# Strassen's seven block products in a feed-forward layer, in two passes over half of F, on one TensorE

## The chip, the cores and the metric

The kernel runs on one core of one Trainium2 chip. The metric is the device time of one execution in microseconds (us); lower is better. A change of 0.2% or less can't be told from no change for this kernel.

## The reference, cut to what matters

One transformer block with cross-attention: B = 16 batches, S = 512 rows, D = 512 features, F = 2048 hidden features, all float32.

```
x   = query + attention(layer_norm(query), context) @ wo + bo
h   = layer_norm(x) * ln2_g + ln2_b
out = x + gelu(h @ w1 + b1) @ w2 + b2        # w1: 512 x 2048, w2: 2048 x 512
```

The change touches only the last two lines, the feed-forward layer.

## The kernel before

The program has two stages, one after the other. Stage A computes the attention for all batches and writes `x` to the DRAM scratch `x1`. Stage B (`stage_b`, lines 840 to 1194) reads it back and computes the feed-forward layer. TensorE (PE) multiplies in the format fp32r, and every product is made of three: each operand is split into a high part (rounded to that format) and a low part (the rest), and `split_product` (lines 952 to 956) adds high x high, high x low and low x high into one PSUM bank. A "high" is a rounding copy, a "low" is one subtraction of two SBUF tiles. The columns streamed by one matmul are 512 in stage B.

Stage B keeps both parts of `w1` and `w2` in SBUF and goes once over the 16 batches. Per batch:

- **Load.** SP loads the batch twice, as `xn` (for the norm) and as `xr` (for the residual) (lines 939 to 942).
- **Norm and transpose.** DVE computes statistics and normalises `xn` (lines 1032 to 1047), PE transposes it in 16 transposes of 128 columns (`x_transpose`, line 958), ACT writes the high part and DVE the low part of `hT` (lines 1121 and 1049). The scale `ln2_g` is folded into `w1` and the shift into `b1` once, at the start (`scale_w1`, line 1069; `bias_product`, line 988).
- **Hidden tiles.** For each of 16 tiles of 128 hidden features (`hidden`, line 966): 12 matmuls into `bank_f`; ACT applies gelu (line 1146); DVE writes the high part (line 1058) and the low part (line 1060) of the result.
- **Output.** Two tiles later (`output`, line 977): 12 matmuls that add this tile's share to the four banks `bank_o`. After the last tile DVE adds `bank_o` to `xr` (line 1113) and SP stores it (line 945). POOL has added `b2` to `xr` before (line 1190).

So a batch is 16 x 12 + 16 x 12 = 384 matmuls of 512 columns and 16 transposes. Each engine has its own program, in which the first batch, a loop over the middle 14 and the last batch are written out; engines meet only at semaphores, and the instructions of one engine start in the order written. During the first batch the weights are split as they come in: `w1` by ACT and DVE (lines 1126 and 1078), `w2` by ACT and POOL (lines 1130 and 1177).

Lines of stage A that the prediction uses only for their durations: line 410 is its dense products (those of V stream 256 columns), 460 and 425 the attention's, 710 the exponential on ACT.

## Time and profile before

| | us |
|---|---|
| median of 3 runs | 3095.35 (3094.23 to 3096.35) |
| the profiled execution: its own time | 3096.19 |
| its span, first to last instruction | 3094.5 |
| stage A | 0 to 1587 |
| stage B | 1587 to 3094.5 |

Busy over the span: PE 96%, weight load (PEld) 78%, DVE 49%, ACT 37%, POOL 15%; mean granted TensorE clock 0.982. The profiled execution is 0.8 us above the median. Its own time is 1.7 us more than its span.

How to read it: "busy" is the time in which at least one instruction of the engine is under way. Matmuls overlap, so the time of one (398 ns for 512 columns) is longer than the distance from its start to the next one's. The views used below are: the table of stretches (busy time of each engine, granted clock, DMA), the chain of work that ended last, the groups of instructions by line, the order in time of one engine, one line's durations, and the page's list of DMA issues.

### The profile page before, as it was taken

Reading aid. Unit: us, or ns where it says so; the run is one execution under the profiler, and the core shown is the slowest. Engines: PE = TensorE matmul, PEld = TensorE weight load, DVE = VectorE, ACT = ScalarE, POOL = GpSimd, SP = SyncE. Lnnn points to the kernel's source line nnn. Section 1 sums busy time; section 2 is a strip of 40 time slices with the busy share of each in tenths; the row PEclk is TensorE's granted clock in tenths of the full one; section 3 lists DMA queues with packets and bytes.
Section 4 is the critical chain, followed back from the end, with each engine's and each line's share of the span. In section 5 each row is a group of like instructions: output and inputs, shape, how many; then the busy total and the mean of one; then the engine's idle time right before and its main releaser. Section 6 shows DMA issues by size and latency. Waiting matters only on the chain. (4 is left out here: it accounts for less than half of the span.)

```text
span 3094.5 us, 52560 instructions
## 1 busy us (share of the span) xinstructions
PE 2965.2 (96%) x17576; PEld 2408.6 (78%) x17576; DVE 1520.4 (49%) x4100; ACT 1153.1 (37%) x2958; POOL 459.1 (15%) x432
## 2 busy tenths in 40 slices
PE   6999999999999999999979999999999999999999
PEld 5777877778777777777758888888888888888887
DVE  4766666666676666766634333322333322333322
ACT  3655566555666565655622111111111111111111
POOL 1222122211222112222112000000000000000000
PEclk9999999999999999999979999999999999999999
DMA  5766676666666666666522111100111100111100
GB/s 133 122 113 102 111 107 111 115 110 108 107 108 119 112 102 115 103 119 110 89 85 82 41 41 41 41 9 32 41 41 41 41 31 10 41 41 41 41 27 14
DMA packets 123695, 231.89 MB, mean 75 GB/s; under 512 B 10752, under 2 KB 10752, under 8 KB 123648
## 3 DMA queue, kind: packets, MB, share of 16 engines
q1 hardware_dynamic: 123648, 231.28, 37.5%
q8 instruction: 28, 0.46, 0.1%
q14 instruction: 19, 0.16, 0.0%
HBM read 97.02 MB, written 33.55 MB: 42 GB/s over the span
## 5 line engine op out<-in xcount | busy, mean ns | idle before, releaser
L710 ACT ACTIVATE sm<-sm,mins 128x128 f32<-128x128 f32 (+3 forms) x1024 | 571.7, 559 | 606.4 <-DVE mins L574 603.6
L574 DVE CUSTOM_DVE_ANT_0 sm<-bank_s,mask 128x128 f32<-128x128 f32 (+3 forms) x1024 | 480.7, 488 | 451.2 <-PE bank_s L425 440.5
L1146 ACT ACTIVATE g_sb<-bank_f,b1s 128x512 f32<-128x512 f32 x256 | 176.2, 688 | 1173.1 <-PE bank_f L956 1173.1
L1058 DVE CAST g_hi<-g_sb 128x512 fp32r<-128x512 f32 x256 | 113.0, 441 | 866.9 <-ACT g_sb L1146 866.9
L437 PE MATMUL bank_t<-ident,sm 128*128 128x128 f32 x2560 | 424.1, 281 | 53.5 <-ACT pT L520 34.1
L437 PEld LDWEIGHTS bank_t<-ident,sm 128*128 128x128 f32 x2560 | 305.8, 143 | 156.9 <-issue 76.6
L954 PE MATMUL bank_f<-hT_hi,w_hi 128*128 128x512 f32 x1024 | 407.6, 398 | 1.6 <-DVE hT_lo L1052 1.6
L954 PE MATMUL bank_o<-w_hi,g_hi 128*128 128x512 f32 x1024 | 408.0, 398 | 0.0
L956 PE MATMUL bank_f<-hT_hi,w_lo 128*128 128x512 f32 x1024 | 406.7, 397 | 0.0
L955 PE MATMUL bank_f<-hT_lo,w_hi 128*128 128x512 f32 x1024 | 406.4, 397 | 0.0
L956 PE MATMUL bank_o<-w_hi,g_lo 128*128 128x512 f32 x1024 | 406.3, 397 | 0.0
L955 PE MATMUL bank_o<-w_lo,g_hi 128*128 128x512 f32 x1024 | 405.6, 396 | 0.0
L425 PE MATMUL bank_s<-stack 96*128 96x128 f32 (+3 forms) x1024 | 357.3, 390 | 6.5 <-DMA stack<-st_lo 5.8
L520 DVE COPY pT<-bank_t 128x384 f32<-128x384 f32 (+1 forms) x576 | 326.9, 568 | 0.5 <-PE bank_t L437 0.5
L1190 POOL TENSOR_TENSOR xr<-xr,b_row 128x512 f32<-128x512 f32 x64 | 81.3, 1301 | 1213.2 <-DMA xr<-x_scratch 1213.2
L954 PEld LDWEIGHTS bank_f<-hT_hi,w_hi 128*128 128x128 f32 x1024 | 193.4, 189 | 48.3 <-issue 2.0
L956 PEld LDWEIGHTS bank_f<-hT_hi,w_lo 128*128 128x128 f32 x1024 | 193.7, 189 | 47.4
L955 PEld LDWEIGHTS bank_f<-hT_lo,w_hi 128*128 128x128 f32 x1024 | 193.9, 189 | 46.8
L956 PEld LDWEIGHTS bank_o<-w_hi,g_lo 128*128 128x128 f32 x1024 | 193.1, 189 | 46.6
L955 PEld LDWEIGHTS bank_o<-w_lo,g_hi 128*128 128x128 f32 x1024 | 193.0, 188 | 46.2
L954 PEld LDWEIGHTS bank_o<-w_hi,g_hi 128*128 128x128 f32 x1024 | 192.8, 188 | 45.5
L792 POOL TENSOR_TENSOR oT_lo<-rT,oT_hi 128x512 fp32r<-128x512 f32 x64 | 82.3, 1286 | 814.6 <-ACT oT_hi L724 814.6
(108 smaller groups left out, 4486.5 us busy)
## 6 DMA issues: line engine op xcount, KB each, us to landing
stack<-st_hi SPq DMA_DIRECT2D x256, 256.0 KB, 5.6
xt<-in_x SPq DMA_DIRECT2D x32, 1024.0 KB, 5.3
stack<-st_lo SPq DMA_DIRECT2D x128, 256.0 KB, 7.2
c_raw<-in_ctxT SPq DMA_DIRECT2D x64, 256.0 KB, 6.0
x_scratch<-xt SPq DMA_DIRECT2D x64, 256.0 KB, 2.0
xn<-x_scratch SPq DMA_DIRECT2D x16, 1024.0 KB, 7.7
xr<-x_scratch SPq DMA_DIRECT2D x16, 1024.0 KB, 5.6
out<-xr SPq DMA_DIRECT2D x64, 256.0 KB, 2.1
```

The source lines that it names most:

```text
L425: mm = pe.matmul(bank_s[n % BANKS_S][:, off:off + w], stack[0:96, g % 2, 0, r, P * qt:P * qt + P], stack[0:96, g % 2, 1, r, 0:w], start=Tr ...
L437: mm = pe.transpose(bank_t[n % 2][:, P * c:P * c + P], sm[:, n % SLOTS_S, P * c:P * c + P], ident[:])
L520: copy(out, src).then_inc(moved[n % 2], 1)
L574: op = V.tensor_tensor_reduce(sm[:, n % SLOTS_S, off:off + w], bank_s[n % BANKS_S][:, off:off + w], mask[:, 512 - w:512], 1.0, 0.0, ALU.ad ...
L710: op = A.activation(row, row, ACT.Exp, bias=mins[:, g % 2, c:c + 1], scale=-1.0, accum_out=sums[:, g % 2, c:c + 1])
L792: G_.tensor_tensor(out=oT_lo[:, g % NG, :], in0=rT[:], in1=oT_hi[:, g % NG, :].bitcast(F32), op=ALU.subtract).then_inc(oT_done, 1)
L954: pe.matmul(o, lh, rh, start=first, stop=False)
L955: pe.matmul(o, lh, rl, start=False, stop=False)
L956: return pe.matmul(o, ll, rh, start=False, stop=last)
L1058: V.tensor_copy(g_hi[:, f % RING_H, :], g_sb[:, f % 2, :]).then_inc(g_hi_ok, 1)
L1146: A.activation(g_sb[:, f % 2, :], bank_f[f % 2][:], ACT.Gelu, bias=b1s[:, f:f + 1], scale=1.0).then_inc(gelu, 1)
L1190: G_.tensor_tensor(out=xr[:, t, :], in0=xr[:, t, :], in1=b2_row[:], op=ALU.add).then_inc(xr_ok, 1)
```

## The change

Matrices are cut into 2 x 2 blocks, and each block product of the feed-forward layer is done by the Strassen-Winograd scheme: seven products of blocks in place of eight, with sums of blocks before and after. Both layers are done so. To make room in SBUF for the seven block operands of `w1` and `w2`, the work is done in two passes over all batches, each with one half of F: pass 0 adds the first half's share of the output and `b2` to `x` and stores it back into the DRAM scratch; pass 1 loads that, adds the second half's share and stores the result. The normalised and transposed `hT` is computed in pass 0, stored to a new DRAM scratch (`h_scratch`) and loaded again in pass 1. One batch in one pass is called a unit here; there are 32.

What a unit does:

- PE, first layer (`layer1`): 14 steps in the order of `STEPS`, as (d, place): d is the half of the unit's hidden features, place one of the seven products. A step is 2 x 2 x 3 = 12 matmuls of 256 columns. In pass 0 four groups of four transposes for the next batch follow steps number 9 to 12; all four use one bank, `bank_t`.
- PE, second layer (`layer2`): k = 0 to 6, the seven products, each in two halves h = 0, 1 of 12 matmuls of 256 columns. `layer2(0)` stands before the last step of the first layer. k = 0, 2, 4 and 6 share `bank_x2`, so k = 4 waits until the output of k = 2 was added to `xr` (`sum_out(2)`).
- ACT: 6 copies of PSUM blocks to `g`, 16 gelus of 128 x 256, 14 highs of the second layer's left operands (`a_high`), 7 highs of the next unit's `h` (`h_high`), in pass 0 also 4 scaled copies that make `hT`.
- DVE: 6 additions PSUM + SBUF (`add`), 8 sums of SBUF blocks (`a_sum`), 8 lows (`a_low`), 4 sums and 4 lows for the next unit's `h` (`h_parts`, stages 0 to 4), 7 additions PSUM + SBUF to `xr` (`sum_out`); in pass 0 also the norm of the next batch.
- POOL: 6 lows (`a_low` of k = 3, 4, 6) and 3 lows of `h` (B22, B21, T3); in pass 0 the four additions of `b2` and the inverse root.
- The weights' block operands are made on the way, in the first unit of pass 0, the last unit of pass 0 and the first unit of pass 1 (`w1_parts`, `w2_parts`: each 7 highs on ACT, 4 sums and 4 lows on DVE, 3 lows on POOL). Their raw blocks are loaded into `xr`, `g` or `xn`, one after the other, as `raw_used` allows.

All blocks are 128 x 512 elements. The core of the diff:

```diff
-def stage_b(nc, x1, w1, w2, vecs, b2, out):
...
+def stage_b(nc, x1, h_scratch, w1, w2, vecs, b2, out):
...
+    STEPS = [(0, 0), (0, 1), (0, 2), (0, 3), (0, 4), (0, 5), (1, 0), (0, 6),
+             (1, 1), (1, 2), (1, 3), (1, 4), (1, 5), (1, 6)]
+    X_AFTER = {9: 0, 10: 1, 11: 2, 12: 3}
...
+    A_LOW_V = [(0, 0), (1, 0), (0, 1), (1, 1), (2, 0), (2, 1), (5, 0), (5, 1)]
+    A_LOW_P = [(3, 0), (3, 1), (4, 0), (4, 1), (6, 0), (6, 1)]
...
+    T_HIGH = ["B11", "B22", "T1", "T3", "B21", "T2", "T4"]
+    T_LOW_V, T_LOW_P = ["B11", "T1", "T2", "T4"], ["B22", "B21", "T3"]
...
+    PLACE1_B = ["B11", "T1", "B21", "T2", "B22", "T3", "T4"]
...
+        b_hi = sb("b_hi", [P, 7, 2, C], F32R)
+        b_lo = sb("b_lo", [P, 7, 2, C], F32R)
...
+        raw = [xr, g[:, 4:8, :], xr, xr, xn, xn, xn, xn]
...
+        def over_batches(eng, body):
...
+            body(0, 0, True, False)
             with eng.Fori(1, B - 1) as c:
+                body(c, 0, False, False)
+            body(B - 1, 0, False, True)
+            body(B, 1, True, False)
+            with eng.Fori(B + 1, 2 * B - 1) as c:
+                body(c, 1, False, False)
...
+            def raw_used(u):
+                sp.wait_ge(w_lo_v, 4 * (u + 1))
+                sp.wait_ge(w_lo_p, 3 * (u + 1))
...
+            def store_h(m):
+                sp.wait_ge(hT_ok, m * KT + KT)
+                sp.dma_start(one(h_v, m), hT[:]).then_inc(h_stored, 16)
...
+            def body(c, ph, first, last):
+                b = c - ph * B
+                if ph == 0 and not last:
+                    sp.wait_ge(x_t, c * KT + KT)
+                    sp.dma_start(xn[:], one(x_v, b + 1)).then_inc(xn_in, 16)
...
+                    sp.wait_ge(stored, c * 32 + 32)
...
+            def x_transpose(m, f, bank):
+                if f == 0:
+                    pe.wait_ge(xn_ok, m * QT + QT)
+                if f > 0 and bank is bank_t:
+                    pe.wait_ge(hT_ok, m * KT + f)
+                for t in range(QT):
+                    mm = pe.transpose(bank[:, P * t:P * t + P], xn[:, t, P * f:P * f + P], ident[:])
...
+            def block_product(o, lh, ll, rh, rl, opens):
+                pe.matmul(o, lh, rh, start=opens, stop=False, skip_group_check=True)
+                pe.matmul(o, lh, rl, start=False, stop=False, skip_group_check=True)
+                return pe.matmul(o, ll, rh, start=False, stop=True, skip_group_check=True)
...
+            def layer1(c, ph, first, d, at_place):
...
+                if at_place == 6:
+                    pe.wait_ge(added, at(c, ADDS, (d, "C22")))
+                for m in range(2):
+                    cols = slice(P * (2 * d + m), P * (2 * d + m) + P)
+                    for kt in range(2):
+                        mm = block_product(bank[:, C * m:C * m + C], w1_hi[:, at_place, kt, cols],
+                                           w1_lo[:, at_place, kt, cols], b_hi[:, at_place, kt, :],
+                                           b_lo[:, at_place, kt, :], at_place < 3 and m == 0 and kt == 0)
+                mm.then_inc(step1, 1)
...
+            def layer2(c, ph, first, k):
...
+                if k == 4:
+                    pe.wait_ge(summed, at(c, OUTPUTS, 2))
...
+                    if (k, h) in A_LOW_V:
+                        pe.wait_ge(a_lo_v, at(c, A_LOW_V, (k, h)))
+                    else:
+                        pe.wait_ge(a_lo_p, at(c, A_LOW_P, (k, h)))
...
+            def body(c, ph, first, last):
+                for n, (d, place) in enumerate(STEPS):
+                    if n == 13:
+                        layer2(c, ph, first, 0)
+                    layer1(c, ph, first, d, place)
+                    if n in X_AFTER and ph == 0 and not last:
+                        x_transpose(c + 1, X_AFTER[n], bank_t)
+                for k in range(1, 7):
+                    layer2(c, ph, first, k)
...
+            def t_parts(n, q, hi, lo, hi_ok, sum_ok, lo_v, lo_p, stage):
+                if stage == 0:
+                    dve.wait_ge(hi_ok, n * 7 + 1)
+                    low(lo("B11"), q["B11"], hi("B11"), lo_v)
+                if stage == 1:
+                    V.tensor_tensor(q["B11"], q["B12"], q["B11"], ALU.subtract).then_inc(sum_ok, 1)
+                    V.tensor_tensor(q["B12"], q["B22"], q["B12"], ALU.subtract).then_inc(sum_ok, 1)
+                if stage == 2:
+                    dve.wait_ge(hi_ok, n * 7 + 3)
+                    low(lo("T1"), q["B11"], hi("T1"), lo_v)
+                    dve.wait_ge(lo_p, n * 3 + 1)
+                    dve.wait_ge(sum_ok, n * 4 + 1)
+                    V.tensor_tensor(q["B22"], q["B22"], q["B11"], ALU.subtract).then_inc(sum_ok, 1)
+                if stage == 3:
+                    dve.wait_ge(lo_p, n * 3 + 2)
+                    dve.wait_ge(sum_ok, n * 4 + 3)
+                    V.tensor_tensor(q["B21"], q["B21"], q["B22"], ALU.subtract).then_inc(sum_ok, 1)
+                    dve.wait_ge(hi_ok, n * 7 + 6)
+                    low(lo("T2"), q["B22"], hi("T2"), lo_v)
+                if stage == 4:
+                    dve.wait_ge(hi_ok, n * 7 + 7)
+                    low(lo("T4"), q["B21"], hi("T4"), lo_v)
...
+            def h_parts(m, ph, stage):
+                if stage == 1 and ph == 0:
+                    dve.wait_ge(h_stored, m * 16 + 16)
...
+            def a_low(c, k, h):
+                dve.wait_ge(a_hi_ok, at(c, A_HIGH, (k, h)))
+                low(a_part(a_lo, k, h), a_source(k, h), a_part(a_hi, k, h), a_lo_v)
...
+                dve.wait_ge(step2, at(c, HALVES, (k, 1)))
+                o = xr[:, 2 * i:2 * i + 2, C * j:C * j + C]
+                V.tensor_tensor(o, bank[:].rearrange("p (t n) -> p t n", t=2), o, ALU.add).then_inc(summed, 1)
...
+            def body(c, ph, first, last):
+                norm = ph == 0 and not last
+                more = ph == 0 or not last
+                if ph == 0 and first:
+                    w2_parts(2, 0, 0)
...
+                add(c, 0, "C11")
+                if norm:
+                    layer_norm_stats(c + 1, 0)
+                    layer_norm_stats(c + 1, 1)
+                add(c, 0, "C12")
+                a_low(c, 0, 0)
+                if norm:
+                    layer_norm_stats(c + 1, 2)
+                add(c, 0, "C22")
+                if norm:
+                    layer_norm_stats(c + 1, 3)
+                a_sum(c, "S1", 0)
+                a_low(c, 1, 0)
+                if norm:
                     for t in range(QT):
+                        normalise(c + 1, t)
+                a_sum(c, "S2", 0)
+                if ph == 0 and first:
+                    w2_parts(3, 0, 1)
+                if ph == 0 and last:
+                    w1_parts(4, 1, 0)
+                if ph == 1 and first:
+                    w2_parts(7, 1, 1)
+                add(c, 1, "C11")
+                add(c, 1, "C12")
+                a_low(c, 0, 1)
+                add(c, 1, "C22")
+                if more:
+                    h_parts(c + 1, ph, 0)
+                a_sum(c, "S1", 1)
+                a_low(c, 1, 1)
+                sum_out(c, ph, 0)
+                a_sum(c, "S2", 1)
+                a_low(c, 2, 0)
+                a_low(c, 2, 1)
+                if more:
+                    if ph == 1 or last:
+                        dve.wait_ge(hT_in, (c - B) * 16 + 32)
+                    h_parts(c + 1, ph if not last else 1, 1)
+                    h_parts(c + 1, ph, 2)
+                a_sum(c, "S3", 0)
+                sum_out(c, ph, 1)
+                a_sum(c, "S3", 1)
+                a_sum(c, "S4", 0)
+                a_sum(c, "S4", 1)
+                if more:
+                    h_parts(c + 1, ph, 3)
+                sum_out(c, ph, 2)
+                a_low(c, 5, 0)
+                sum_out(c, ph, 3)
+                a_low(c, 5, 1)
+                if more:
+                    h_parts(c + 1, ph, 4)
+                for k in (4, 5, 6):
+                    sum_out(c, ph, k)
+                if ph == 0 and last:
+                    w1_parts(5, 1, 1)
...
+            def body(c, ph, first, last):
...
+                    h_high(c + 1, "B11")
+                a_high(c, 1, 1)
+                if more:
+                    h_high(c + 1, "B22")
+                a_high(c, 2, 0)
+                activate(c, ph, 1, "C21")
+                a_high(c, 2, 1)
+                if more:
+                    h_high(c + 1, "T1")
+                    h_high(c + 1, "T3")
+                a_high(c, 3, 0)
+                if more:
+                    h_high(c + 1, "B21")
+                a_high(c, 3, 1)
+                if more:
+                    h_high(c + 1, "T2")
+                a_high(c, 4, 0)
+                a_high(c, 4, 1)
+                if more:
+                    h_high(c + 1, "T4")
...
+            def body(c, ph, first, last):
...
+                if ph == 0 and not last:
                     inverse_root(c + 1)
...
+                    pool.wait_ge(xr_in, c * 16 + 16)
+                    for t in range(QT):
+                        G_.tensor_tensor(out=xr[:, t, :], in0=xr[:, t, :], in1=b2_row[:], op=ALU.add).then_inc(xr_ok, 1)
+                if more:
+                    h_low(c + 1, "B22")
+                a_low(c, 3, 0)
+                a_low(c, 3, 1)
+                if more:
+                    h_low(c + 1, "B21")
+                a_low(c, 4, 0)
+                if more:
+                    h_low(c + 1, "T3")
+                a_low(c, 4, 1)
+                a_low(c, 6, 0)
+                a_low(c, 6, 1)
...
```

## Rows read from the trace of the kernel before

**Rows 1.** Stretches: us, busy by engine (instructions), PEclk, DMA share, GB/s.

```profile
1587.00:3094.50 1507.50, 1490.16 (x6528) 1205.73 (x6528) 467.41 (x872) 226.43 (x329) 119.55 (x87) 0.99 0.11 39
1803.39:1894.84 91.45, 91.45 (x402) 73.84 (x401) 27.87 (x53) 13.16 (x20) 6.28 (x5) 1.00 0.10 35
```

**Rows 2.** Chain that ended last, stage B: start us, us, what.

```profile
1609.95 0.77 PE bank_f L954
...
1711.93 0.87 PE bank_x L963 x8
...
1803.39 0.87 PE bank_x L963 x8
...
1894.84 0.87 PE bank_x L963 x8
```

**Rows 3.** PE in order of time, full clock: start us, us, engine, line, what.

```profile
101.92 0.28 PE L410 MATMUL bank_d<-wv_hi,cT_hi 128*128 128x256 f32 x1
...
103.22 0.28 PE L410 MATMUL bank_d<-wv_hi,cT_lo 128*128 128x256 f32 x1
...
1803.23 1.03 PE L963 MATMUL bank_x<-identb,xn 128*128 128x128 f32 x8
...
1804.34 0.39 PE L955 MATMUL bank_o<-w_lo,g_hi 128*128 128x512 f32 x1
...
1806.67 0.39 PE L956 MATMUL bank_o<-w_hi,g_lo 128*128 128x512 f32 x1
```

**Rows 4.** Groups by line, each shape apart: busy us, mean ns, idle before.

```profile
L1146 ACT ACTIVATE g_sb<-bank_f,b1s 128x512 f32<-128x512 f32 x256 | 176.2, 688 | 1173.1 <-PE bank_f L956 1173.1
L1060 DVE TENSOR_TENSOR g_lo<-g_sb,g_hi 128x512 fp32r<-128x512 f32 x256 | 178.3, 697 | 8.8
L1046 DVE TENSOR_SCALAR xn<-xn,mvb,rstdb 128x512 f32<-128x512 f32 x64 | 35.5, 558 | 2.6 <-POOL rstdb L1167 2.6
L1190 POOL TENSOR_TENSOR xr<-xr,b_row 128x512 f32<-128x512 f32 x64 | 81.3, 1301 | 1213.2 <-DMA xr<-x_scratch 1213.2
...
L710 ACT ACTIVATE sm<-sm,mins 128x512 f32<-128x512 f32 x256 | 185.2, 723 | 215.1 <-DVE mins L574 213.1
L710 ACT ACTIVATE sm<-sm,mins 128x256 f32<-128x256 f32 x256 | 126.4, 494 | 0.0
L724 ACT CAST oT_hi<-rT 128x512 fp32r<-128x512 f32 x64 | 38.7, 604 | 2.2 <-DVE rT L584 2.2
```

**Rows 5.** In order of time, three queues: several in one row start one behind another.

```profile
1810.88 2.48 DVE L1113 TENSOR_TENSOR xr<-bank_o,xr 128x512 f32<-128x512 f32 x4 [1.44 <-PE bank_o L956]
1803.86 1.07 ACT L1123 CAST hT_hi<-bank_x 128x512 fp32r<-128x512 f32 x2 [2.55 <-PE bank_x L963]
1822.29 5.05 POOL L1190 TENSOR_TENSOR xr<-xr,b_row 128x512 f32<-128x512 f32 x4 [85.24 <-DMA xr<-x_scratch]
```

**Rows 6.** DVE and POOL in order of time, where they meet in the first batch.

```profile
1693.51 1.79 DVE L1060 TENSOR_TENSOR g_lo<-g_sb,g_hi 128x512 fp32r<-128x512 f32 x1
1695.23 1.51 DVE L1046 TENSOR_SCALAR xn<-xn,mvb,rstdb 128x512 f32<-128x512 f32 x1
...
1693.47 5.66 POOL L1190 TENSOR_TENSOR xr<-xr,b_row 128x512 f32<-128x512 f32 x4
```

**Rows 7.** The page's DMA issues: KB each, us to landing.

```profile
xn<-x_scratch SPq DMA_DIRECT2D x16, 1024.0 KB, 7.7
xr<-x_scratch SPq DMA_DIRECT2D x16, 1024.0 KB, 5.6
```

**Rows 8.** PE in order of time behind two idle times, stage A.

```profile
37.40 0.39 PE L410 MATMUL bank_d<-wv_hi,cT_hi 128*128 128x256 f32 x1 [2.16 <-DVE wv_lo L606]
...
38.16 0.41 PE L410 MATMUL bank_d<-wv_hi,cT_lo 128*128 128x256 f32 x1
...
41.15 0.41 PE L410 MATMUL bank_d<-wv_lo,cT_hi 128*128 128x256 f32 x1
...
116.94 0.76 PE L410 MATMUL bank_d<-xnT_hi,wq_hi 128*128 128x512 f32 x1 [1.70 <-DVE xnT_lo L552]
```

More of the change, by code:

```diff
@@ L950, in _ @@
+            over_batches(sp, body)
+            sp.wait_ge(stored, 64 * B + 32)
         @block.tensor
         def _(pe):
[L952 to L964 removed]
@@ new lines, in _ @@
+            pe.sem_inc(step1, len(STEPS))
+            pe.sem_inc(step2, len(HALVES))
+            pe.wait_ge(consts, 1)
+            for f, bank in enumerate((bank_x2, bank_y2, bank_z2, bank_t)):
+                x_transpose(0, f, bank)
+            def body(c, ph, first, last):
[7 more added lines that the diff above has]
+                    layer2(c, ph, first, k)
@@ new lines, in h_high, with copy @@
+            def h_high(m, name):
+                act.wait_ge(step1, before(m, STEPS, (1, PLACE1_B.index(name))))
+                t_high(m + 1, quarters(hT), lambda name: b_hi[:, PLACE1_B.index(name), :, :], b_hi_ok, b_sum_ok, name)
+            def copy(c, d, name):
+                place, bank, to = {"P1": (0, bank_x[d], "C11"), "P5": (1, bank_y, "C22"), "U2": (3, bank_x[d], "C12")}[name]
+                act.wait_ge(step1, at(c, STEPS, (d, place)))
+                A.copy(g_block(d, to), bank[:].rearrange("p (m s) -> p m s", m=2)).then_inc(copied, 1)
@@ new lines, in activate @@
+            def activate(c, ph, d, name):
+                rows = "C1 C2".split().index(name[:2])
+                if name == "C21":
+                    act.wait_ge(step1, at(c, STEPS, (d, 6)))
+                else:
+                    act.wait_ge(added, at(c, ADDS, (d, name)))
+                for m in range(2):
+                    to = g_block(d, name)[:, m, :]
+                    f = 2 * KT + 8 * ph + 4 * rows + 2 * d + m
+                    op = A.activation(to, bank_x[d][:, C * m:C * m + C] if name == "C21" else to, ACT.Gelu,
+                                      bias=vec[:, f:f + 1], scale=1.0)
+                op.then_inc(gelu, 1)
@@ L1183, in body @@
-            def body(c, first, last):
-                if first:
-                    for wc in range(WC):
-                        w2_low(wc)
-                    inverse_root(1)
-                pool.wait_ge(xr_in, c * 16 + 16)
-                for t in range(QT):
-                    G_.tensor_tensor(out=xr[:, t, :], in0=xr[:, t, :], in1=b2_row[:], op=ALU.add).then_inc(xr_ok, 1)
-                if not last and not first:
-                    inverse_root(c + 1)
-            over_chunks(pool, body)
+            w1_parts(0, 0, 0)
```

609 lines of the change are left out of this document (395 added, 214 removed).

## The prediction

> **What bounds it now.** The table of stretches says that stage B takes 1507.5 of 3094.5 us, and that in a middle batch PE is busy for all of its 91.45 us at full clock, DVE for 27.9, ACT for 13.2, POOL for 6.3 [rows 1]. The chain of waits shows the same from the other side: its pieces in stage B are matmuls one behind another, and the transposes come back every 91.45 us [rows 2]. So only fewer or shorter matmuls help, and PE has no idle time to lose: what the other engines add is free only while it stays under PE. The first batch is dearer: 102.0 us from its first matmul to its transposes [rows 2], where a middle batch needs 84.1 (a period less the 24 matmuls and 16 transposes that close it, 7.4); so the weights and the start cost 17.9 us.
>
> **PE's work.** The distance between matmuls is read at full clock: ten distances of 512 columns take 2.33 us; eleven of 256 columns 1.30 us, so 118.2 ns each [rows 3]. Eight transposes take 0.88 us with the step back to matmuls (1803.23 to 1804.34, less one matmul), so 16 cost 1.8 [rows 3]. That leaves (91.45 - 1.8) / 384 = 233.5 ns per 512 columns over a whole batch. After: 672 x 0.1182 = 79.4 us, plus 2.0 for the transposes in four groups. PE's work falls from 91.45 to 81.4, by 10.1 us a batch, 161 us in all. Splitting 512 columns into 256 costs nearly nothing: the weights' load keeps up in the V products, which load as often. A pass-1 unit is 336 x 0.1182 = 39.7 us of PE, a pass-0 unit 41.6.
>
> **The other engines.** DVE: 0.69 us for 128 x 512, and one behind another every 0.60 (four in 2.48). ACT: 0.60 for a high, 0.58 for a copy, every 0.49 (two in 1.07); a gelu of 256 columns 0.49, as the exponential of that shape from SBUF (of 512 columns it takes 0.72 and the gelu 0.69). POOL: 1.29, every 1.25 (four in 5.05) [rows 4, 5]. Per unit: DVE 37 x 0.60 = 22 (pass 0: 27), ACT 20 (22), POOL 9 x 1.25 = 11 (17). All are under 39.7: no engine is full, and if throughput were all, the change would give its 161 us. What decides is the order, because PE now meets the others many times a unit, and they meet one another.
>
> **DVE against POOL.** In the first batch, a DVE low (both inputs in SBUF), 0.69 elsewhere, started 0.04 behind the first of POOL's four additions and took 1.79: it ended 0.54 after POOL's first one did (1693.47 + 1.29 = 1694.76; 1695.30). DVE's next, a normalise (0.56 elsewhere), took 1.51 and ended about 0.27 after POOL's second. The four additions took 5.66 in place of 5.05: the 0.6 are DVE's turn [rows 5, 6]. So in this trace they take turns by whole instructions. The Trainium skill (SBUF — State Buffer, section Who interferes with whom) says of which this holds: a VectorE instruction with two SBUF inputs and a GpSimd instruction that reads SBUF block each other for the whole instruction, one with a single SBUF input isn't touched; the trace agrees for the one low it can show. The page speaks against this change, which puts 24 two-input DVE instructions beside 9 POOL lows in a unit; by it the sum is 3425, without it 3127 (below). I take turns for all of them, as the row shows for the same kind of instruction: a pair costs 1.25 + 0.54 = 1.79, less 0.04 of overlap. DVE's additions with an input in PSUM I leave free; if they took turns too, the two in the stretch below would cost 1 to 2 us a unit.
>
> **The walk of a unit.** I went through the five queues in the order of the diff, starting each instruction when its queue is free and its last wait over, with the durations above and as allowances, which no row fixes closely, 0.04 to 0.15 us from one engine to the next and 0.11 more when PE starts again (0.05 more each way is worth 20 us in all). It repeats after one unit. The long stretch is the end of the second layer. Call T the end of DVE's low of (k 2, h 1). DVE then has, before it may add the output of k = 2 (for which k = 4 waits, bank_x2): sums T1 and T3, low T1, sum T2 (to T + 2.6), sums S3(0), S3(1), S4(0), S4(1), sum T4, low T2, and two additions to xr. POOL is released at T + 2.4 by the high of (3, 0), and from there has six lows in a row: (3, 0), (3, 1), B21, (4, 0), T3, (4, 1). Each of DVE's six meets one of them: 6 x 1.75 = 10.5. Sum T4 also has to wait for B21. The addition of k = 2 ends at T + 13.55, PE starts k = 4 at T + 13.7. In that time PE has only the halves (2, 1), (3, 0), (3, 1): 4.3 us. Idle: 0.4 at k = 2, 1.6 and 0.2 at k = 3 (POOL's lows), 6.5 at k = 4, and 0.45 for four starts: 9.2. **A pass-1 unit takes 48.9.**
>
> **Pass 0** has in addition: the load of xn is issued only behind the last store of the unit before (1.6 us after PE began the unit), lands 5.6 later [rows 7], and DVE wanted it at 5.1; the addition C22 comes late and step (0, 6) waits 1.2. The normalise starts behind it, together with POOL's four additions of b2, and three of its four take turns with them: PE waits 4.6 for the first transposes. The four groups share one bank: 0.7 and 0.65 for ACT's copies. With the 8.3 of the second layer and 0.8 for seven starts: 16.3. **A pass-0 unit takes 57.9.** A batch is then 57.9 + 48.9 = 106.8 where it was 91.45. DVE's wait for the store of hT costs nothing: it lands 4 to 5.6 us after its issue and DVE comes 6.3 after it (at 7.7, PE would lose 1.4 a unit).
>
> **The ends.** To the first matmul 27 (now 23). First unit 84, 26 more than a middle one: two blocks of w2 come one after the other (5.6 load, then some 10 of sums and lows) and stand in DVE's queue before the additions that PE waits for. The boundary unit 58.7 (two blocks of w1 in place of the norm). First unit of pass 1 74.1, 25 more, again two blocks of w2. Sum of stage B: 27 + 84 + 14 x 57.9 + 58.7 + 74.1 + 14 x 48.9 + 43.8 (the last, nothing to prepare) + 1 = 1784; with 1587 before it 3371.
>
> **The clock.** Behind an idle time of 2.16 us the matmuls of 256 columns stand 0.214 us apart from 38.16 to 41.15 (14 distances in 2.99), where 0.107 would be full speed by their columns: the granted clock is at 1.2 in place of 2.4 GHz, for some 3.4 us. Behind 1.70 us the first matmul takes 0.76 in place of 0.39, the same fall [rows 8]. A unit's 6.5 us are longer than either, and PE is then the bound until the next unit's middle. I take 1.7 us for each of 32 units: 54. Bounds: none (0), or twice in a pass-0 unit (+27). Sum: 3371 + 54 = 3425 span, 3427 with the 1.7 around it; the profiled execution is 0.8 above the median: 3426.
>
> **Rivals.**
> 1. *Turns and half clock*, as above: 3426. Own range 3290 (DVE at 0.60 and 0.51, which the walk prices at -78, and little half clock) to 3485 (xn landing in 7.7, +30, and two falls a unit). For it: [rows 6, 8]. Chance 0.65; with full clock all through, 3371: 0.12.
> 2. *No turns*: the low of row 6 was an accident. The same walk without them gives 49.1 and 43.3 a unit (idle 1.5 at k = 4, 1.35 at the transposes) and 3127 in all; up to 3180 with half clocks. Slower still, since the queues' order alone eats the gain. Against: three instructions in [rows 6] agree to 0.1 us. Chance 0.10.
> 3. *Faster*: the queue behind T drains in time. The place is `sum_out(2)` against k = 4: if it ends within PE's 4.3 us, and the norm likewise, PE never waits: 1587 + 23 + 16 x 81.4 + 18 + 25 + 5 = 2960. The other ends cost some 37 us more than now, 2.3 a batch, so it decides at an idle time of 10.1 - 2.3 = 7.8 us a batch; the walk has 25. For it: no engine is over 70% full by throughput. Against: six POOL lows at 1.25 alone are 7.5 us, longer than 4.3. Chance 0.11.
> 4. *Seven blocks are no cheaper than eight*: in long runs 256 columns are held up by the weights' load. At the 184 ns a load that PEld's busy time gives (73.84 / 401, [rows 1]), PE's work alone would be 125.6 a batch: about 3680. Against: the 12 in a row at 118 [rows 3]. Chance 0.02.
>
> **The numbers.** 3426 is the likeliest. The range 3150 to 3480 leaves out the faster case, the lower half of rival 2, and rival 4. Faster by over 0.2% (what can be told from no change) 0.11, slower 0.86, between 0.03.
>
> **What would show it.** Right: PE busy some 80% in stage B and waiting longest for DVE's addition to xr; DVE's two-input instructions at 1.2 to 1.8 us in the mean of their groups, POOL's lows at 1.6 to 1.8; 256-column matmuls 118 ns apart; granted clock near 0.96 in stage B. Wrong: POOL's lows at 1.29 (no turns), PE's idle under 8 us a batch, a clock of 1.00 behind the long waits, or matmuls over 125 ns apart.

## The result, and the profile after

The changed kernel takes 3465.7 us (median of 4 runs, 3464.2 to 3466.9) where the kernel before took 3095.7 in the same session: a ratio of 1.119 (95% interval 1.118 to 1.121). It is slower by 370 us; 3426 was forecast, with a range of 3150 to 3480. The profiled execution has a span of 3464.9.

The stretches of [rows 1] in the profile after, first all of stage A and all of stage B, then one unit of pass 0 and one of pass 1 (columns as there: PE, weight load, DVE, ACT, POOL, granted clock, DMA share, GB/s):

```profile
0.00:1587.00 1587.00, 1475.47 (x11048) 1202.22 (x11048) 1052.76 (x3228) 927.11 (x2629) 339.86 (x345) 0.98 0.63 109
1587.00:3464.90 1877.90, 1463.55 (x11008) 1431.55 (x11008) 1140.68 (x1456) 784.34 (x1497) 582.06 (x395) 0.90 0.19 67
2193.47:2254.87 61.40, 47.21 (x355) 45.70 (x354) 37.85 (x50) 24.89 (x47) 20.76 (x14) 0.92 0.20 68
2702.06:2753.04 50.98, 43.28 (x339) 42.55 (x338) 30.02 (x37) 21.99 (x43) 13.56 (x9) 0.93 0.18 63
```

Stage A is what it was. Stage B takes 1877.9 in place of 1507.5. PE works 1463.6 us there: less than the 1490.2 of before even with the stretches at half clock counted in, and it now waits for the other 414. DVE has gone from 467 to 1141 us of busy time, POOL from 120 to 582.

What PE waited for in stage B (engine, line, tile <- releaser: us in total, times, longest us). Before, the middle batches had no such waits: PE was busy for all of their 91.45 us [rows 1]:

```profile
PE bank_x L1080 <- DVE xr L1304: 191.3, 31, 6.2
...
PE bank_t L1069 <- DVE xn L1192: 65.0, 15, 4.5
...
PE bank_z L1080 <- POOL a_lo L1560: 44.5, 31, 1.5
```

The first row is the wait of k = 4 for DVE's addition of k = 2, 31 times 6.2 us; the second is the transposes' wait for the normalise, 4.3 us each; the third k = 3 behind POOL's lows. These are the three places that the walk named, at nearly the lengths it gave (6.5, 4.6, 1.6). Left out above are the waits of the first units (47.4 us in 6 waits for ACT's copies, L1439) and one more that the walk named, step (0, 6) behind DVE's addition of C22 (L1267): 21.1 us in 14 waits, 1.5 each, where it had 1.2.

The groups that answer to [rows 4] (busy us, mean ns), POOL's lows, DVE's sums and its normalise, and one of its additions with an input in PSUM:

```profile
L1560 POOL TENSOR_TENSOR a_lo<-g,a_hi 128x512 fp32r<-128x512 f32 x192 | 287.6, 1505 | 352.2 <-ACT a_hi L1464 352.0
...
L1560 POOL TENSOR_TENSOR b_lo<-hT,b_hi 128x512 fp32r<-128x512 f32 x96 | 151.0, 1573 | 603.5 <-ACT b_hi L1421 603.5
...
L1284 DVE TENSOR_TENSOR s_sums<-g,s_sums 128x512 f32<-128x512 f32 x64 | 110.3, 1762 | 0.0
...
L1279 DVE TENSOR_TENSOR g<-g 128x512 f32<-128x512 f32 x64 | 93.2, 1456 | 0.0
...
L1304 DVE TENSOR_TENSOR xr<-bank_x,xr 128x512 f32<-128x512 f32 x128 | 87.8, 686 | 164.1 <-PE bank_x L1082 164.1
...
L1192 DVE TENSOR_SCALAR xn<-xn,mvb,rstdb 128x512 f32<-128x512 f32 x64 | 71.2, 1171 | 1.1 <-POOL rstdb L1557 1.1
...
L1243 DVE TENSOR_TENSOR hT<-hT 128x512 f32<-128x512 f32 x32 | 55.8, 1744 | 1.2 <-POOL b_lo L1560 1.2
```

The same kind of instruction costs 0.69 us where nothing meets it [rows 4], and 1.74 to 1.76 in the mean of the two groups whose every member meets POOL (s_sums, L1284, and hT, L1243). Additions with one input in PSUM (L1304) stay at 0.69 in the midst of the same stretch. One such stretch in a pass-0 unit, in order of time:

```profile
2169.99 1.46 DVE L1196 TENSOR_TENSOR a_lo<-s_sums,a_hi 128x512 fp32r<-128x512 f32 x2
...
2173.94 1.78 DVE L1279 TENSOR_TENSOR g<-g 128x512 f32<-128x512 f32 x1
2175.64 0.68 DVE L1304 TENSOR_TENSOR xr<-bank_y,xr 128x512 f32<-128x512 f32 x1
2176.24 1.18 DVE L1279 TENSOR_TENSOR g<-g 128x512 f32<-128x512 f32 x1
2177.35 3.45 DVE L1284 TENSOR_TENSOR s_sums<-g,s_sums 128x512 f32<-128x512 f32 x2
2180.72 1.74 DVE L1243 TENSOR_TENSOR hT<-hT 128x512 f32<-128x512 f32 x1
2182.39 1.75 DVE L1196 TENSOR_TENSOR b_lo<-hT,b_hi 128x512 fp32r<-128x512 f32 x1
2184.07 0.68 DVE L1304 TENSOR_TENSOR xr<-bank_x,xr 128x512 f32<-128x512 f32 x1
```

```profile
2173.90 2.98 POOL L1560 TENSOR_TENSOR a_lo<-g,a_hi 128x512 fp32r<-128x512 f32 x2 [4.38 <-ACT a_hi L1464]
2176.84 1.75 POOL L1560 TENSOR_TENSOR b_lo<-hT,b_hi 128x512 fp32r<-128x512 f32 x1
...
2181.88 1.71 POOL L1560 TENSOR_TENSOR a_lo<-g,a_hi 128x512 fp32r<-128x512 f32 x1
```

```profile
2184.80 0.58 PE L1080 MATMUL bank_x<-w_hi,a_hi 128*128 128x256 f32 x1 [6.17 <-DVE xr L1304]
```

T, the end of DVE's low of (2, 1), is 2169.99 + 1.46 = 2171.45 here. DVE's six meetings with POOL are the rows of 1.78, 1.18, 3.45 (two instructions), 1.74 and 1.75 in the first list, POOL's six lows run from 2173.90 to 2183.59 in the second (two of them left out), and PE's first matmul of k = 4 begins at T + 13.35, where T + 13.7 was forecast.

### The profile page after: what moved, and what is told of

It reads as the page before. It is cut to its first block, busy times and chain, and to the rows that moved or that the text cites. A ratio compares the mean times of both kernels' runs of the same rounds, so it can differ in the third digit from the quotient of the medians.

```text
span 3464.9 us, 66386 instructions
## 1 busy us (share of the span) xinstructions
PE 2939.0 (85%) x22056; PEld 2633.8 (76%) x22056; DVE 2193.4 (63%) x4684; ACT 1711.5 (49%) x4126; POOL 921.9 (27%) x740
## 4 chain that ended last, share of the span: by engine, by line
PE 24%; DVE 18%; issue 5%; ACT 4%; DMA 3%; DVEq 0%; SPq 0%; POOL 0%; ACTq 0%
PE bank_x L1080 5%; PE bank_x L1081 5%; PE bank_x L1082 5%; DVE s_sums L1284 3%; DMA xn<-x_scratch 3%; DVE g L1279 2%; DVE xr L1304 2%; PE bank_y L1080 2%; PE bank_y L1081 2%; PE bank_y L1082 2%; DVE xn L1192 2%; DVE hT L1243 1%; ACT a_hi L1464 1%; DVE b_lo L1196 1%; ACT b_hi L1421 1%
## 5 line engine op out<-in xcount | busy, mean ns | idle before, releaser
L1080 PE MATMUL bank_x<-w_hi,a_hi 128*128 128x256 f32 x1024 | 331.2, 323 | 192.6 <-DVE xr L1304 191.3
L1080 PEld LDWEIGHTS bank_x<-w_hi,a_hi 128*128 128x128 f32 x1024 | 229.3, 224 | 202.8 <-DVE xr L1304 197.5
L1560 POOL TENSOR_TENSOR a_lo<-g,a_hi 128x512 fp32r<-128x512 f32 x192 | 287.6, 1505 | 352.2 <-ACT a_hi L1464 352.0
L1080 PE MATMUL bank_x<-b_hi,w_hi 128*128 128x256 f32 x1024 | 305.7, 299 | 78.9 <-ACT g L1439 47.4
L1081 PE MATMUL bank_x<-w_lo,a_hi 128*128 128x256 f32 x1024 | 321.4, 314 | 0.0
L1082 PE MATMUL bank_x<-w_hi,a_lo 128*128 128x256 f32 x1024 | 319.1, 312 | 0.0
L1081 PE MATMUL bank_x<-b_lo,w_hi 128*128 128x256 f32 x1024 | 300.8, 294 | 0.0
L1082 PE MATMUL bank_x<-b_hi,w_lo 128*128 128x256 f32 x1024 | 300.7, 294 | 0.0
L1081 PEld LDWEIGHTS bank_x<-w_lo,a_hi 128*128 128x128 f32 x1024 | 230.6, 225 | 0.0
L1082 PEld LDWEIGHTS bank_x<-w_hi,a_lo 128*128 128x128 f32 x1024 | 229.2, 224 | 0.0
```

The lines of the kernel that those rows point to most:

```text
L1080: pe.matmul(o, lh, rh, start=opens, stop=False, skip_group_check=True)
L1081: pe.matmul(o, lh, rl, start=False, stop=False, skip_group_check=True)
L1082: return pe.matmul(o, ll, rh, start=False, stop=True, skip_group_check=True)
L1560: G_.tensor_tensor(out=out_, in0=value, in1=high.bitcast(F32), op=ALU.subtract).then_inc(sem_, 1)
```

## The experiments

Each was timed against the kernel before on the same chip. The walk of the prediction, now with 1.9 us of half clock behind each of PE's waits over 1.7 us, gives 3459 for the changed kernel; the forecasts below are differences from that.

**1. The addition of k = 2 put earlier in DVE's queue.**

```diff
                 sum_out(c, ph, 1)
+                sum_out(c, ph, 2)
                 a_sum(c, "S3", 1)
...
-                sum_out(c, ph, 2)
                 a_low(c, 5, 0)
```

> DVE's addition of the output of k = 2 stands right behind that of k = 1, ahead of the sums S3(1), S4(0), S4(1), sum T4 and low T2; nothing else is changed, and the same is computed. Turns with the half clock (my theory; the walk of the record with 1.9 us of half clock behind each idle time over 1.7 us gives 3459 for the changed kernel, 3466 was measured): the wait of k = 4 goes from 6.5 to 2.0 us and is then one for POOL's low of (4, 0), a second of 1.9 us may stand at (4, 1); a pass-1 unit takes 47.3 in place of 51.0, in all 3351, so 108 less than the changed kernel's walk: 3358. Rival A, no turns, POOL is only slow by itself: the wait for this addition would be 1.5 us long, and moving it gives at most 1.5 us a unit: 3415 or more. Rival B, what is lost is lost to the clock alone: a unit's half clock stays as long as any wait is left, and no more than the 4 us of idle time a unit is gained with the clock still at 0.90.

Measured: 3360.1 us, ratio 1.0845 (1.083 to 1.086); 3358 was expected. What PE waited for in stage B:

```profile
PE bank_x L1080 <- POOL a_lo L1560: 102.7, 62, 1.9
...
PE bank_x L1080 <- DVE xr L1304: 16.2, 27, 0.6
```

The 31 waits of 6.2 us are gone, and 62 of at most 1.9 for POOL's low stand in their place, twice a unit. The first pass-1 units take 47.5 (from one store of xr to the next), the later ones 48.7 and 47.0 in turn. Rival A falls, since 105 us were gained where it allowed 50. Rival B falls by the clock: stage B has a granted clock of 0.94 in place of 0.90. The time alone would not have told, for 105 us are 3.3 a unit and B allowed 4. This place in the queue was worth 105 us: PE's waits at k = 4 fell by 72 in all (191.3 to 102.7 + 16.2), and most of the rest is half clock that is gone.

Behind these waits the clock does not always fall. In the unit around 2780 the matmuls behind a wait of 1.87 us are 0.12 us apart; in the unit around 3065 those behind one of 1.86 us fall to 0.21 apart after the second distance.

**2. The additions of b2 moved to pass 1.**

```diff
-                    if ph == 0:
-                        dve.wait_ge(xr_ok, c * QT + QT)
+                    if ph == 1:
+                        dve.wait_ge(xr_ok, (c - B) * QT + QT)
...
-                if ph == 0:
+                if ph == 1:
                     if first:
                         pool.wait_ge(b2_in, 16)
```

> POOL's four additions of b2 to xr are made in pass 1 in place of pass 0, so they no longer stand beside the normalise; the same is computed, and the number of instructions stays. Turns: the wait of the transposes in pass 0 falls from 4.7 to 1.5 us and its half clock goes with it; a pass-0 unit 56.6 in place of 61.1, a pass-1 unit 51.8 in place of 50.8 (its own DVE instructions meet the four additions); in all 3410 by the walk whose value for the changed kernel is 3459, so 49 less: 3417. Rival, no turns: the normalise is late because its data are (the wait is there for the load of xn), and nothing changes: 3466, with DVE's normalise at 1.17 us in the mean as now.

Measured: 3417.2, ratio 1.1035 (1.102 to 1.105); 3417 was expected. DVE's normalise:

```profile
L1192 DVE TENSOR_SCALAR xn<-xn,mvb,rstdb 128x512 f32<-128x512 f32 x64 | 31.5, 555 | 1.1 <-POOL rstdb L1557 1.1
```

0.555 us each, as in [rows 4], where it was 1.17 (above), and PE's wait for it at bank_t falls from 65.0 to 16.5 us in all: the load was not what made it late.

**3. PE kept busy through the wait of k = 4.**

```diff
+                if k == 4:
...
+                    fill(48)
```

(`fill` runs 48 matmuls of 256 columns from w2_hi into bank_t; in pass 0 it waits first until ACT has read that bank)

> Ahead of the wait of k = 4, in every unit, PE runs 48 more matmuls of 256 columns on weights that lie ready, into bank_t, which nobody reads then (48 x 0.118 = 5.7 us, where the wait is 6.2). They compute nothing that is used. The clock: if an idle PE is what takes the clock to one half, the fall at k = 4 goes away in both passes; the matmuls behind it stand 0.12 us apart at once, the granted clock over stage B goes from 0.90 to 0.96 or more, and the time falls by about 1.9 x 30 = 57 us to 3410 (3400 to 3425). Rival: the half clock does not hang on the idle time at k = 4 (it comes with the load on the chip, or costs less than I think): 3466 or more, and a clock of 0.90.

Measured: 3410.9, ratio 1.1015 (1.0996 to 1.103), 55 below the changed kernel; 3410 was expected. Stage B:

```profile
1587.00:3408.10 1821.10, 1586.35 (x12544) 1552.55 (x12544) 1141.37 (x1456) 784.20 (x1497) 584.62 (x395) 0.96 0.20 69
```

The granted clock is 0.96 in place of 0.90, although every engine but PE has the same work as before. So the half clock at k = 4 is the consequence of PE's idle time, and costs 55 / 32 = 1.7 us a unit. In the changed kernel it can be seen in PE's own rows behind the wait:

```profile
2185.61 0.41 PE L1080 MATMUL bank_x<-w_hi,a_hi 128*128 128x256 f32 x1
...
2188.81 0.37 PE L1080 MATMUL bank_x<-w_hi,a_hi 128*128 128x256 f32 x1
```

Between these two there are 15 distances of 0.213 us, which is 1.2 GHz for 256 columns; from 2189.02 on they are 0.12 apart, at 2.4 GHz.

**4. POOL's lows of the second layer in two halves.**

```diff
-                low(a_part(a_lo, k, h), a_source(k, h), a_part(a_hi, k, h), a_lo_p)
+                for m in range(2):
+                    op = G_.tensor_tensor(out=a_part(a_lo, k, h)[:, m, :], in0=a_source(k, h)[:, m, :],
+                                          in1=a_part(a_hi, k, h)[:, m, :].bitcast(F32), op=ALU.subtract)
+                op.then_inc(a_lo_p, 1)
```

> POOL makes each of its six lows of the second layer as two instructions of 128x256 in place of one of 128x512; the same is computed, in the same order. Turns by whole instructions: DVE gets in after each half, so two of its instructions go by in the time of one low; DVE's two-input groups fall from 1.46 to 1.76 us to about 1.1 to 1.3, the wait of k = 4 goes from 6.5 to 2.0, that of k = 3 from 1.6 to 2.1, a pass-1 unit takes 48.4, in all 3384 by the walk whose value for the changed kernel is 3459, so 75 less: 3390. Rival A, no turns (POOL and DVE slow each other down in proportion, by sharing bandwidth): the halves take as much time together as the whole does, DVE's instructions stay at 1.5 to 1.75 us, and the time is 3466 or, with a fixed cost for each of 6 more POOL instructions a unit, up to 3490.

Measured: 3426.0, ratio 1.106 (1.104 to 1.109). 40 us are gained, where turns by whole instructions gave 75 and a sharing of bandwidth none.

```profile
L1284 DVE TENSOR_TENSOR s_sums<-g,s_sums 128x512 f32<-128x512 f32 x64 | 75.4, 1217 | 0.0
...
L1279 DVE TENSOR_TENSOR g<-g 128x512 f32<-128x512 f32 x64 | 60.8, 950 | 0.0
```

```profile
L1586 POOL TENSOR_TENSOR a_lo<-g,a_hi x384: 715/1168/1257, 1682.8 to 3415.5; 128x256 fp32r<-128x256 f32 x192
```

```profile
PE bank_x L1080 <- DVE xr L1304: 75.9, 31, 3.0
...
PE bank_z L1080 <- DVE xr L1304: 62.8, 31, 2.1
```

(The third row gives the least, median and longest duration of POOL's halves in ns, the last two are PE's waits.) DVE's two-input sums fell from 1.76 and 1.46 to 1.22 and 0.95 us: it does get in between the halves. But a half takes 0.72 at the least, more than half of a whole low's 1.29 [rows 4], and 1.17 in the median, so the two take longer than the whole low did here (1.50). The wait of k = 4 stays at up to 3.0 where 2.0 was expected; the one at k = 3 is 2.1 long, as expected, but for DVE's addition and not for POOL's low. The direction is the turns'; the size was missed.

**5. All nine lows on DVE, near their old places.** POOL's body loses its nine calls and DVE's gets them; `t_op` is one instruction of the old `h_parts`, and the counts that PE waits for change over with them.

```diff
+                    t_op(c + 2, H_Q, H_HI, H_LO, b_hi_ok, b_sum_ok, b_lo_v, B_LOW_V, "sT2")
+                a_low(c, 3, 0)
                 a_sum(c, "S3", 0)
                 sum_out(c, ph, 1)
+                a_low(c, 3, 1)
                 a_sum(c, "S3", 1)
                 a_sum(c, "S4", 0)
                 a_sum(c, "S4", 1)
...
-                a_low(c, 3, 0)
-                a_low(c, 3, 1)
```

> All nine of POOL's lows of a unit (six of the second layer, B22, B21, T3 of h) are made by DVE, each put into DVE's queue near where its high is ready; the rest of the order and POOL's four additions of b2 stay. The same is computed. Turns: a low on POOL costs 1.25 us there and holds one of DVE's for as long, on DVE it costs 0.60: so DVE gets nine more instructions and its unit still becomes shorter. By the walk the wait of k = 4 goes from 6.5 to 4.0 us (DVE is now simply full of work there), k = 3 keeps 1.2 to 1.5, a pass-1 unit takes 47.7, a pass-0 unit 58.1, in all 3361. Signs: no DVE two-input group over 0.72 us beside the normalise. Rival, no turns: DVE loses what POOL did for it, 9 x 0.6 = 5.4 us more in front of the additions that PE waits for, and the time rises over 3466.

Measured: 3367.6, ratio 1.088 (1.086 to 1.090); 3361 was expected. DVE's groups:

```profile
L1198 DVE TENSOR_TENSOR a_lo<-g,a_hi 128x512 fp32r<-128x512 f32 x256 | 172.3, 683 | 0.2
...
L1198 DVE TENSOR_TENSOR a_lo<-s_sums,a_hi 128x512 fp32r<-128x512 f32 x192 | 139.3, 726 | 81.3 <-ACT a_hi L1519 78.3
...
L1194 DVE TENSOR_SCALAR xn<-xn,mvb,rstdb 128x512 f32<-128x512 f32 x64 | 71.3, 1173 | 1.1 <-POOL rstdb L1614 1.1
```

The engine that already had the longest queue was given nine more instructions a unit and the kernel became 98 us faster. All of DVE's groups of this shape with two SBUF inputs are at 0.68 to 0.73 in the middle units; the normalise alone, which still meets POOL's additions of b2, is at 1.17.

**6. Everything on DVE and the queues in a new order.** Beyond run 5, b2 is added by DVE in pass 1, the load of xn is issued a unit earlier, and DVE's and ACT's bodies are reordered. DVE's queue from the low of (2, 1) on, as it now stands:

```python
                a_low(c, 2, 1)
                a_low(c, 3, 0)
                a_sum(c, "S4", 1)
                a_low(c, 3, 1)
                sum_out(c, ph, 1)
                a_low(c, 4, 0)
...
                sum_out(c, ph, 2)
...
                a_low(c, 5, 0)
                a_low(c, 4, 1)
                sum_out(c, ph, 3)
...
                a_low(c, 5, 1)
                a_low(c, 6, 0)
...
                sum_out(c, ph, 4)
```

Where lines are left out, a sum or a low of h fills in. S3(0), S3(1) and S4(0) come earlier, ahead of low (2, 1), and the last three lows of h stand around the addition of k = 5. ACT's highs were reordered likewise, those of the second layer ahead of those of h that nobody needs yet.

> A version meant to beat both: all lows on DVE as in the run before, the four additions of b2 on DVE too and in pass 1, DVE's and ACT's queues put into an order found with the walk (each addition to xr right when its product is done, the sums and lows of the first layer's next operand filled in behind), and xn loaded one unit earlier. The same is computed. Turns gone, order mended: by the walk PE has no wait over 0.3 us in a middle unit, a pass-0 unit takes 41.7 and a pass-1 unit 39.7, the first units of the passes 68 and 65, in all 2980: 0.962 of the kernel before. DVE is at 78 to 85% there. Rival A: seven products of 256 columns are dearer on PE than 118.2 us per thousand (the changed kernel shows 0.1195 to 0.12 apart in places), which adds up to 1.5%: 3015. Rival B: a full DVE makes each handover late by a little, with 20 handovers a unit of 0.1 us each: 3045. Slower than 3095 would say that the order's gain is not what the walk holds it for.

Measured: **3011.7 us, ratio 0.973 (0.971 to 0.974)**: faster than the kernel before by 86 us and than the changed one by 454. Stage B and a pass-1 unit:

```profile
1587.00:3010.40 1423.40, 1346.95 (x11008) 1338.22 (x11008) 1086.32 (x1808) 782.56 (x1497) 57.62 (x43) 0.97 0.26 89
2627.22:2667.54 40.32, 40.32 (x338) 40.32 (x337) 30.87 (x52) 22.00 (x44) 0.00 (x0) 1.00 0.22 78
```

PE is busy for all of the 40.32 us of the unit, at full clock, with DVE at 30.9 beside it. 40.32 / 336 = 120.0 ns a matmul, not 118.2: rival A of the expectation, +19 us over the kernel. A pass-0 unit takes 43.0 where 41.7 was expected: the pitch (the distance from one matmul to the next) again, +0.6, and 0.7 for the transposes and small waits. The dear units are the boundary unit (47.4 from one store of xr to the next) and the first of pass 1 (66.7).

**7. The same order with the nine lows back on POOL.**

> The run before with one thing undone: the nine lows are on POOL again, in the same order, all else in the new order. The same is computed. Turns: POOL's lows each hold one of DVE's sums or lows; by the walk a pass-1 unit takes 44.6 and a pass-0 unit 46.6, PE waits 1.9 us for DVE's low of the second layer, with half clock behind it, in all 3133, that is 153 above the run before. Rival, no turns: DVE has nine instructions fewer and PE has no wait: 2958, a little below the run before.

Measured: 3057.7, ratio 0.9875 (0.986 to 0.989): 46 us above run 6, where strict turns gave 153 and none gave -22, and still 40 us faster than the kernel before. PE's waits for POOL's lows are 23.5 us in all, those for DVE's lows 16.3 (7.4 in run 6). The trace shows one place where the walk was too dear. DVE, then POOL, in order of time:

```profile
2659.21 0.68 DVE L1310 TENSOR_TENSOR s_sums<-g,s_sums 128x512 f32<-128x512 f32 x1
2659.81 0.68 DVE L1201 TENSOR_TENSOR a_lo<-s_sums,a_hi 128x512 fp32r<-128x512 f32 x1
2660.41 0.68 DVE L1310 TENSOR_TENSOR s_sums<-g,s_sums 128x512 f32<-128x512 f32 x1
2661.02 0.68 DVE L1330 TENSOR_TENSOR xr<-bank_y,xr 128x512 f32<-128x512 f32 x1
```

```profile
2659.26 6.00 POOL L1623 TENSOR_TENSOR a_lo<-g,a_hi 128x512 fp32r<-128x512 f32 x3 [26.23 <-ACT a_hi L1525]
```

POOL's low came 0.05 us behind DVE's sum at 2659.21, and DVE's next two followed it at their usual 0.60. So it was POOL that waited: its three lows took 6.00 us in place of 3.75. Taken singly they are 3.00, 1.30 and 1.78 us: the first ended at 2662.26, which is its usual 1.25 behind the start of DVE's addition with a PSUM input (2661.02). The walk had DVE wait at each meeting. That the new order also has more slack for the waits that are left is my reading, and no run separates the two.

**8. By hand.** As run 6, but with ACT's queue untouched and DVE's only mended at single places.

> The changed kernel with the single steps put together by hand, and ACT's queue left as it is: all lows on DVE, b2 added by DVE in pass 1, xn loaded a unit earlier, each addition to xr put right behind its product, and the lows T1, T2, T3, T4 of h behind the last lows of the second layer. The same is computed. With nobody on POOL and DVE at 0.60 an instruction, the walk (with 120 ns a matmul, as e6_reordered showed) gives 49.7 for a pass-0 unit and 48.9 for a pass-1 unit, 3256 in all: six waits a unit of 0.6 to 1.7 us, most for DVE's lows, are left because ACT's order still hands DVE its highs late. e6_reordered differs from it only in the order of DVE's and ACT's queues. If taking POOL off and earlier additions were nearly all of it, the time would be close to e6_reordered's 3012, under 3080.

Measured: 3234.7, ratio 1.044 (1.042 to 1.046); 3256 was expected. Run 6 is 223 us faster with the same instructions on the same engines: that much is the order of DVE's and ACT's queues. Reordering the two together doesn't say how much is due to each.

**9. Spare POOL work beside run 6.**

```diff
+                for n, (k, h) in enumerate([(3, 0), (3, 1), (4, 0), (5, 0), (4, 1), (5, 1), (6, 0), (6, 1), (6, 1)]):
+                    pool.wait_ge(a_hi_ok, at(c, A_HIGH, (k, h)))
...
+                    G_.tensor_tensor(out=spare[:], in0=b2_row[:], in1=b2_row[:], op=ALU.subtract)
```

> e6_reordered with nine spare POOL instructions of 128x512 in each unit, where e7_reordered_pool has its lows: they subtract b2 from itself into a tile nobody reads, two SBUF inputs, and no engine waits for them. What is computed stays. So any time above e6_reordered's 3012 is what POOL costs DVE by being in its way, with POOL's own lateness left out. Theory A, strict turns (each DVE two-input instruction that meets POOL waits for it, as the walk has it): 3290. Theory B, who is there first keeps the path: DVE's instructions that follow one another at 0.60 hold POOL off until one with an input in PSUM or a gap comes, and DVE waits only where POOL came first: by the walk with that rule 3052 (3040 to 3070), POOL's instructions at 1.7 us in the mean with some near 3. Theory C, e7_reordered_pool's 46 us were PE waiting for POOL's own lows and DVE loses nothing: 3012.

Measured: 3188.9, ratio 1.0295 (1.028 to 1.031), 177 above run 6. Theory C falls: work that nobody waits for costs 5.5 us a unit, by being in DVE's way. PE's waits for DVE's additions to xr and its lows are 136 us in all (70.9, 47.7, 12.1 and 5.6), where run 6 has 7.4. It costs more than run 7's lows did, although the spare instruction is shorter (1.04 us at the least): DVE now has the nine lows as well. A is 101 too dear and B 137 too cheap, and the rows say what lies between. DVE, then POOL:

```profile
2670.25 0.68 DVE L1311 TENSOR_TENSOR s_sums<-g,s_sums 128x512 f32<-128x512 f32 x1
...
2672.66 0.68 DVE L1202 TENSOR_TENSOR a_lo<-g,a_hi 128x512 fp32r<-128x512 f32 x1
2673.26 0.68 DVE L1331 TENSOR_TENSOR xr<-bank_y,xr 128x512 f32<-128x512 f32 x1
2673.86 0.93 DVE L1202 TENSOR_TENSOR a_lo<-g,a_hi 128x512 fp32r<-128x512 f32 x1
2674.71 1.52 DVE L1202 TENSOR_TENSOR b_lo<-hT,b_hi 128x512 fp32r<-128x512 f32 x1
```

```profile
2670.39 12.54 POOL L1694 TENSOR_TENSOR spare<-b_row 128x512 f32<-128x512 f32 x7 [30.39 <-ACT a_hi L1538]
```

POOL asked at 2670.39, 0.14 behind a DVE sum. Five two-input instructions of DVE, from 2670.25 to 2672.66, then ran at 0.60 us apart; the first with an input in PSUM came at 2673.26. From there on DVE's take 0.93 and 1.52, as these two do. POOL's first took 3.86 us by itself, which is 1.04 from 2673.21 on: it came in with DVE's PSUM addition, as in run 7. In both places DVE kept POOL out as long as it had not been made to wait itself; once POOL had been let in, they took turns. That this is the rule everywhere is not shown.

## Why the prediction was right, and where it was not

**PE's work.** 672 matmuls a batch are cheaper than 384 of 512 columns, as said; run 6, at 3011.7, shows 86 us of it (its first units keep the rest). The price was 118.2 ns, read off eleven distances; over whole units it is 120.0 (run 6): 16 x 672 x 1.8 ns = 19 us too low.

**Turns.** Right, in kind and nearly in size: 1.74 to 1.76 us for DVE's instructions that all meet POOL (1.79 less 0.04), PSUM inputs free. POOL's lows were to be at 1.6 to 1.8 and are at 1.50 and 1.57; the first of a row comes before DVE and takes 1.27 (the one at 2173.90). Rival 2 (no turns) falls with runs 2, 5 and 9. Where DVE is first, the walk was wrong: it had DVE wait at each meeting, and in runs 7 and 9 DVE's instructions kept POOL out while they followed one another.

The Trainium skill (SBUF — State Buffer, section Who interferes with whom) states an exclusive lock of the shared ports for a VectorE instruction with two SBUF inputs and a GpSimd instruction that reads SBUF, and the trace after agrees, down to the exemption of additions with a PSUM input (0.686 us). It exempts an instruction with one SBUF input only outside the two-port modes, and names `tensor_scalar` among the operations that can enter them; the prediction left this condition out. The normalise is such an instruction and does take turns: 1.51 us in [rows 6], 1.17 in the profile after and 0.555 in run 2, where POOL's additions were moved away. Whether it ran in a two-port mode no run shows. The forecast did not suffer, since the walk counted three of its four as meeting POOL.

**The walk.** The three waits stand where it put them. A unit was to take 57.9 and 48.9 without the clock; measured are 61.45 and 51.16 (means of 14 units in each pass), the boundary unit 61.9 for 58.7 and the first unit of pass 1 78.6 for 74.1, from one store of xr to the same of the next unit. The walk took 5.6 us for the load of xn, where [rows 7] has 7.7 for it, without saying why; the profile after has 5.7, so this held by a choice that was not argued. What a unit takes over the walk is the clock's, less 0.6 for the pitch:

**The clock** is the term that was furthest off. I took 54 us, one fall a unit at k = 4, and run 3 confirms it: 55. But pass 0 has a second one behind the transposes' wait, which I had as a bound and not in the sum. PE in the profile after:

```profile
2155.09 1.12 PE L1069 MATMUL bank_t<-identb,xn 128*128 128x128 f32 x4 [4.50 <-DVE xn L1192]
2155.85 0.56 PE L1080 MATMUL bank_x<-b_hi,w_hi 128*128 128x256 f32 x1
...
2158.14 0.36 PE L1081 MATMUL bank_x<-b_lo,w_hi 128*128 128x256 f32 x1
...
2158.45 0.60 PE L1069 MATMUL bank_t<-identb,xn 128*128 128x128 f32 x4
2158.81 0.36 PE L1080 MATMUL bank_y<-b_hi,w_hi 128*128 128x256 f32 x1
```

Four transposes take 0.76 us from start to start of what follows (2155.09 to 2155.85), at full clock 0.36 (2158.45 to 2158.81): 0.4. Ten distances between matmuls make 2.29, at full clock 1.20: 1.1. That is 1.5 in each of 15 units, 22 us. By unit the walk is then 57.9 + 1.7 + 1.5 + 0.6 = 61.7 (61.45 measured) and 48.9 + 1.7 + 0.6 = 51.2 (51.16). With both the sum is 3371 + 55 + 22 + 19 = 3467, beside 3464.9; the granted clock of stage B is 0.90 where I wrote 0.96.

**Rival 3** (faster) was priced at 2960 with PE never waiting. The change as made is far from it; run 6 comes within 52 us of it, 19 of them the pitch. What I had against it, six POOL lows at 1.25 in a row, was right for this order of the queues only: run 7 has the same nine lows on POOL and takes 3057.7.

**Where the expected gain went.** PE's work fell by 91.45 - (40.32 + 42.97) = 8.2 us a batch, 130 in all, if run 6's two units, in which it hardly waits, are taken for it. In its place came 6.2 us a unit at k = 4, 4.3 at the transposes, 1.5 at k = 3 and the half clock behind them. Of the 454 us between the changed kernel and run 6, taking POOL's lows away is worth 98 alone (run 5), the other single steps and DVE's mended places another 133 (run 8), and the new order of DVE and ACT the last 223. These shares hold for this sequence of steps: with the new order already made, taking the lows from POOL is worth 46 (run 7 against run 6).

What stays open: which rule of turns gives the 3188.9 of run 9 (strict turns gave 3290, first come 3052), what besides its length decides whether a wait takes the clock down, and how much of the 26 us by which the first unit of pass 1 is dearer in run 6 could be hidden.

## What to carry to other kernels

A change that makes the bounding engine's work shorter by adding work to the others has to come with a new order of their queues: put the instruction that frees a bank for the bounding engine right behind the product it reads, and fill in the rest behind it. Do not give GpSimd two-input work out of SBUF to relieve a VectorE that is itself full of such work: in the new order the kernel is 46 us faster with the nine lows on DVE, where they occupy it for 9 x 0.60 = 5.4 us a unit, and in the old order 98 us. Nine spare instructions on POOL beside them cost 5.5 us a unit without doing anything. The order of the queues counts for more than this choice: 223 us (run 8 against run 6). Price the half clock for each long wait of PE, not once for each unit, and as a range where the wait is under some 2 us: it fell behind 1.70 us in [rows 8], not behind 1.75 us in the profile after (PE at 2207.35), and both ways behind 1.86 and 1.87 us in run 1.

## What the runs showed of the hardware

- Matmuls of 256 columns follow one another at 120.0 ns over a whole unit (336 in 40.32 us), those of 512 at 233.5 [rows 3]: the shorter form costs 2.8% more for the same columns.
- In two places DVE's two-input instructions that ran back to back held a GpSimd instruction off until an addition with a PSUM input began: 1.7 us in run 7 (its first low 3.00, alone 1.29), 2.8 in run 9 (3.86, alone 1.04).
- A GpSimd subtraction of 128x256 takes 0.72 us at the least, where half of the 128x512's 1.29 would be 0.65.
- PE kept busy with unused matmuls through a wait of 6.2 us held the clock at 2.4 GHz there and was worth 1.7 us a wait (run 3: stage B's granted clock 0.96 for 0.90).
- The length of a wait alone did not decide the clock: behind 1.87 us (run 1, 2780.11) it stayed at 2.4 GHz, behind 1.86 us (run 1, 3065.68) it fell to 1.2.
